# One layer of sigmoid attention and routed experts on one core: batch 6's routing moved between batch 7's two value halves, with 30 idle matmuls ahead of the last logits

## The reference, cut to what matters

```python
def reference(x, ctx_2048, g_xattn, g_ffn, norm_w, gate_w, gate_b, w1, b1, w2, b2):
    # x is (8, 256, 512): batch, rows, features; 16 experts, 4 chosen for each row
    q = _layernorm(x)
    score = sigmoid(einsum('bdn,bdm->bnm', q, ctx) / sqrt(256))
    x = x + tanh(g_xattn[0]) * einsum('bvn,bnm->bvm', ctx, score)

    y = _layernorm(x).reshape(2048, 512)
    t = y * rsqrt(mean(y * y) + EPS) * norm_w
    logits = t @ gate_w.T + gate_b
    vals, idx = top_k(logits, 4)
    G = zeros((2048, 16)).at[rows, idx].set(softmax(vals))
    h = einsum('mh,eoh->emo', t, w1) + b1
    a, b = minimum(h[..., ::2], LIMIT), clip(h[..., 1::2], -LIMIT, LIMIT)
    act = a * sigmoid(ALPHA * a) * (b + 1)
    yo = einsum('emi,edi->emd', act, w2) + b2
    return x + tanh(g_ffn[0]) * (y + einsum('me,emd->md', G, yo))
```

## Time and profile before

| what | value |
|---|---|
| median of 3 runs | 813.47 us (811.11 to 813.86) |
| the profiled execution's own time | 812.08 us |
| its span, first to last instruction | 810.3 us |
| mean granted TensorE clock | 0.976 of full speed |
| PE busy | 761.9 us, 94% of the span |
| DVE, ACT, POOL busy | 462.2, 417.3, 303.9 us |

### The profile page before, as it was taken

How to read it: one execution, slowest core, us unless ns; L and a number is a source line. 1 busy time by engine, 2 the same in 40 slices (tenths; PEclk the granted TensorE clock), 3 DMA queues, 4 the chain that set the end, 5 groups by cost and what they waited for, 6 DMA issues and landing times.

```text
span 810.3 us, 16543 instructions
## 1 busy us (share of the span) xinstructions
PE 761.9 (94%) x4067; PEld 651.7 (80%) x4068; DVE 462.2 (57%) x927; ACT 417.3 (51%) x691; POOL 303.9 (38%) x287
## 2 busy tenths in 40 slices
PE   8999996289999999999998999999999999999993
PEld 3666665168889889988888888999999889999892
DVE  3899886336556653556556553746546374735531
ACT  4567663036546554556456544646545364745531
POOL 0157767622342423341423423435333233435212
PEclk9999997599999999999999999999999999999997
DMA  8657743235757656456749654656635465654323
GB/s 285 224 186 235 243 139 117 45 105 157 168 129 209 147 147 158 94 146 200 155 128 234 170 107 136 159 140 155 155 38 151 122 168 142 168 129 77 40 26 40
DMA packets 107768, 117.02 MB, mean 144 GB/s; under 512 B 11808, under 2 KB 77344, under 8 KB 107744
## 3 DMA queue, kind: packets, MB, share of 16 engines
q1 hardware_dynamic: 88896, 77.32, 31.0%
q0 software_dynamic: 18848, 39.40, 25.1%
HBM read 88.06 MB, written 28.94 MB: 144 GB/s over the span
## 4 chain that ended last, share of the span: by engine, by line
PE 80%; DMA 5%; issue 5%; DVE 3%; POOL 3%; ACT 2%; ACTq 1%; DVEq 0%; POOLq 0%
PE ps L553 39%; PE ps L500 22%; PE ps L408 7%; PE ps L396 5%; PE ps L479 4%; DMA xg<-rows,srcI 3%; POOL tab L1181 2%; POOL out L1258 1%; PE ps L425 1%; PE ps L391 1%; PE ps L416 1%; DVE hv L1107 1%; PE ps L589 1%; DVE W1l L1116 1%; DMA ys<-rows,src 1%
## 5 line engine op out<-in xcount | busy, mean ns | idle before, releaser
L553 PE MATMUL ps<-xTh,W1h 128*128 x768 | 256.5, 334 | 4.1 <-issue 3.9
L553 PE MATMUL ps<-xTh,W1l 128*128 x768 | 250.4, 326 | 0.0
L553 PE MATMUL ps<-xTl,W1h 128*128 x768 | 250.3, 326 | 0.0
L1258 POOL DMA_INDIRECT out<-ys,dgI x75 | 118.4, 1579 | 296.4 <-ACT ys L732 277.0
L553 PEld LDWEIGHTS ps<-xTh,W1h 128*128 128x128 f32 x768 | 144.6, 188 | 11.3 <-issue 6.5
L553 PEld LDWEIGHTS ps<-xTh,W1l 128*128 128x128 f32 x768 | 144.6, 188 | 5.2
L553 PEld LDWEIGHTS ps<-xTl,W1h 128*128 128x128 f32 x768 | 144.8, 189 | 4.7
L732 ACT ACTIVATE ys<-ps,dgI 128x512 f32<-128x512 f32 x75 | 51.7, 690 | 133.3 <-DVE ps L1078 133.3
L500 PE MATMUL ps<-W2h,hTh 128*128 x288 | 112.5, 391 | 0.7 <-DVE hTl L1111 0.7
L500 PE MATMUL ps<-W2l,hTh 128*128 x288 | 112.4, 390 | 0.0
L500 PE MATMUL ps<-W2h,hTl 128*128 x288 | 112.2, 390 | 0.0
(11 more groups left out here) (153 smaller groups left out, 974.3 us busy)
## 6 DMA issues: line engine op xcount, KB each, us to landing
W1f<-in_wts SPq DMA_DIRECT2D x64, 512.0 KB, 4.7
W2f<-in_wts SPq DMA_DIRECT2D x32, 512.0 KB, 6.6
X<-in_x SPq DMA_DIRECT2D x8, 512.0 KB, 6.6
Kt<-in_ctx SPq DMA_DIRECT2D x8, 512.0 KB, 4.4
Vt<-in_ctxT SPq DMA_DIRECT2D x8, 512.0 KB, 4.5
rows<-tt SPq DMA_DIRECT2D x8, 512.0 KB, 3.0
out<-base SPq DMA_DIRECT2D x8, 512.0 KB, 2.9
b2s<-in_bias SPq DMA_DIRECT2D x16, 256.0 KB, 8.4
```

Of the source, the lines that this page charges most:

```text
L553: m = e.matmul(P_[i % 2][:, 0:32 * w], (W1h, W1l)[wl][:, i, 2 * k + h, :], (xTh, xTl)[xl][:, bass.ds(par, 1), k, 0:32 * w], start=(t == 0) ...
L1258: e.indirect_dma_start(out, bass.IndirectOffsetOnAxis(dgI[:, j, 0:1].bitcast(I32), axis=0), ys[j][:], None, compute_op=ALU.add).then_inc(d ...
```

## The change

On PE, `av` may now be issued in parts, and the last batch is written out: `av(7, 0)` is split around `turn_t(6)`, `logits(6)` follows it, then three of the four matmuls of `av(7, 1)`, `rank(6)`, the fourth matmul, and 30 idle matmuls ahead of `turn_t(7)`. On ACT, `out_base(6)` goes behind `keep_tT(6)`. On DVE, `choose(6)`, `gates(6)` and `places(6)` go between the two tiles of batch 7. On POOL, the first two of `put(6)`'s eight DMAs go ahead of `x1_scale(7)`.

```diff
-            def av(b, j):
-                if j == 0:
+            def av(b, j, cs=range(4)):
+                if j == 0 and cs[0] == 0:
                     e.wait_ge(d_v[b % 2], 16 * (b // 2 + 1))
                 if b >= 1:
                     e.wait_ge(v_x1, 2 * (b - 1) + j + 1)
-                for c in range(4):
+                for c in cs:
                     if j == 0:
                         e.wait_ge(a_sig, 4 * b + c + 1)
                     m = e.matmul(ps[2 + j][:], Vt[b % 2][:, c, 128 * j:128 * j + 128], Sc[:, c, :], start=(c == 0), stop=(c == 3))
-                m.then_inc(t_av, 1)
+                if cs[-1] == 3:
+                    m.then_inc(t_av, 1)
...
                 qk(b, 3)
+                if b == B - 1:
+                    break
                 av(b, 0)
...
+            av(B - 1, 0, range(2))
+            turn_t(B - 2, 0)
+            turn_t(B - 2, 1)
+            av(B - 1, 0, range(2, 4))
+            logits(B - 2)
+            av(B - 1, 1, range(3))
             rank(B - 2)
+            av(B - 1, 1, range(3, 4))
+            run_idle(30)
             turn_t(B - 1, 0)
             turn_t(B - 1, 1)
             logits(B - 1)
...
-                if b >= 1:
+                if 1 <= b < B - 1:
                     out_base(b - 1, 0)
                     out_base(b - 1, 1)
...
+            out_base(B - 2, 0)
+            out_base(B - 2, 1)
             gate_sigmoids(B - 2)
...
                     if j == 0 and b + 1 < B:
                         low_q(b + 1)
+                    elif j == 0:
+                        choose(B - 2)
+                        gates(B - 2)
+                        places(B - 2)
                 x1_var(b)
-            choose(B - 2)
-            gates(B - 2)
-            places(B - 2)
             base_scale(B - 1)
...
-            def put(b):
+            def put(b, qs=range(2 * K)):
...
-                for q in range(2 * K):
+                for q in qs:
...
+            put(B - 2, range(2))
             x1_scale(B - 1)
-            put(B - 2)
+            put(B - 2, range(2, 2 * K))
             put(B - 1)
```

## The result

| | before | changed |
|---|---|---|
| median | 813.33 us (811.11 to 813.86, 4 runs) | 819.37 us (818.65 to 821.70, 4 runs) |
| ratio | 1 | 1.0078 (95% interval 1.0051 to 1.0106) |
| profiled execution: time, span | 812.08, 810.3 us | 818.65, 816.9 us |
| mean granted TensorE clock | 0.976 | 0.981 |
| PE busy | 761.9 us | 773.6 us |

The change makes the kernel 6.0 us slower; 818.8 us was forecast, with 6.2 us on the path. A later group of runs gave the same ratio, 1.0079 (1.0061 to 1.0097), with 816.90 us against 810.34. All later runs were made in three groups, each beside its own runs of the kernel before (811.15, 810.34 and 810.90 us); each is compared with those of its own group, not with 813.33.

What follows compares the result with a forecast made beforehand. PE is 94% busy; the last put, behind batch 7's path and POOL's queue, sets stage two's start. 2.5 (scaling) + 6.1 (idle matmuls) - 2.2 (warm clock) = +6.4, less up to 0.46: +6.2 on 812.6, 818.8 us; range 815.5 to 822.0.

Steps and rivals of the forecast that it cites:

- transposes could have started: On PE, batch 7's transposes have their scaled input at 137.16 us instead of 134.65, because x1_scale(7) starts 2.5 us later.
- The idle matmuls: On PE, 30 calls of 0.433 us take 13.0 us; 14 exceed the gap and delay batch 7's transposes by 6.1 us.
- Rival A: On PE, idle calls cost up to 0.22 us and just fill the gap: -0.1 to +0.3 us, 812.7 us; chance 0.07.
- the gap figure of the Trainium skill: 0.109 us for a warm 256-column matmul on PE; 30 would take 3.3 or 6.6 us and fit the gap.
- Batch 7's logits: On PE, from first transpose to choose(7) takes 3.25 us at warm clock against 5.48 cold, giving back 2.2 us.
- POOL: Put(6) begins at 133.0 instead of 135.50, but two of its puts delay x1_scale(7) by 2.5 us to 135.24.
- The two bounds of put(7): Batch 7's gates (145.33) and POOL's end of put(6) (145.38) lie close, so shortening POOL's queue alone gains nothing.
- Rival D: At the start of stage two, a wait not moving with the table swallows part: +3 to +4.5, 816 us; chance 0.04.

Runs made afterwards that it cites:

- e8: The changed kernel itself run and profiled again, nothing altered: 816.90 us against 810.34, ratio 1.0079.
- e1: The changed kernel without its 30 idle matmuls, the moved routing kept: 812.25 us against 811.15, ratio 1.0011.
- e2: The changed kernel with 15 idle matmuls instead of 30: 810.95 us against 811.15, ratio 0.9986.
- e3: The changed kernel with 45 idle matmuls instead of 30: 1159.19 us, ratio 1.427.
- e6: The kernel before, order kept, with 8 idle matmuls ahead of rank(6) and 3 behind it: 809.42 us against 810.34, ratio 0.9993.
- e4: The kernel before with only 30 idle matmuls added between rank(6) and batch 7's transposes: 821.38 us against 811.15, ratio 1.0123.
- e7: The changed kernel with tile 1's value matmuls together, 14 idle matmuls, one put ahead of x1_scale(7), gates(7) ahead of places(7): 808.83 us, ratio 0.9986.
- e9: The changed kernel with 30 idle matmuls of 16 columns instead of 30 of 256: 819.88 us, ratio 1.0108.
- e10: The changed kernel with 94 idle matmuls of 16 columns instead of 30 of 256: 845.61 us, ratio 1.0425.
- e5: The changed kernel with 45 idle matmuls of 16 columns instead of 30 of 256: 1149.15 us, ratio 1.418.

## Why the prediction was right

By its own steps, with the second profile of the changed kernel (e8):

| step | predicted | measured |
|---|---|---|
| idle block | 130.34 to 143.3 | 130.35 to 143.31 |
| price of a call | 0.433 us | 0.432 us |
| transposes could have started | 137.16 | 136.68 (e1) |
| choose(7) starts | 146.55 | 146.64 |
| put(6) ends, then POOL waits | 143.9, 8 us | 143.34, 8.78 us |
| put(7) starts later by | 6.0 to 6.4 | 6.04 |
| SP loads the table | 163 | 163.07 |
| time | +6.2 | +6.04 and +6.56 (medians, two groups) |

**The idle matmuls** were the term that decided, and its row was the one that was read right: the start of the next group, not the number of records. Rival A (a call at half its price, the block over before 137.16) is excluded by 0.432 us a call in e2, e3 and e8. By the same rows the gap figure of the Trainium skill ("TensorE: Matmul & The Clock Gate", section "Back-to-back issue gap") does not hold for these float32 calls.

**Batch 7's logits** came back by 2.2 us with the warm clock as forecast: e1 shows 1.97 and 3.57, e2 1.10 and 1.93 for the same transposes and logits at the same place, which start at 136.68 and 136.67, and put(7) starts 2.18 us earlier in e2.

**POOL** was mis-sized by a little. The step "POOL is through with put(5) at 132.71" took over a date from the kernel before; in the changed order it was 131.97 (e8 has the eighth put at 131.02, for 0.95). The second put of batch 6 then took 1.19 instead of 0.96, and `x1_scale(7)` started at 134.75 instead of 135.24. The transposes' input was ready 0.5 us earlier than I said. It changed nothing, since the idle block covered it, but without the block the moved routing cost 1.6 us at put(7), not the 2.1 to 2.5 of e1's expectation.

**The two bounds of put(7)** are shown by e6 (gates at 142.6, put(7) at 145.53) and by the changed kernel (put(6) ends at 143.3, put(7) at 152.12). The 0.29 to 0.75 us from gates to put was 0.76 (gates end at 151.13 + 0.23).

**Rival D, part of the shift is swallowed,** was given 0.04 and is half true: the mechanism is there, the forecast had put it at nothing ("Nothing in the rows shows such a wait"), and the medians did not follow it. In e8 the first transposes of stage two start 6.36 us later than before, and the first matmul of the loop 4.86 later (174.86 against 170.00). The rows of the kernel before and of e8, from their timelines of PE:

```profile
170.00 0.47 PE L553 MATMUL ps<-xTh,W1h 128*128 x1 [1.60 <-issue]
```

```profile
174.86 0.46 PE L564 MATMUL ps<-xTh,W1h 128*128 x1 [0.27 <-DVE xTl L1067]
```

The kernel before has a pause of 1.60 us there that the changed one has not. e6 has it too (1.41), and e1 one of 0.98; the nine other traces wait 0.26 or 0.27 us there. The three with the pause are those with 0 or 11 idle calls, and the others have 14 or more. What the instruction queue did fits that. Its row in the kernel before, for 166.5 to 167.0 us:

```profile
q8 instruction: 1, 0.02, 15.2%
```

So a packet of instructions starts some 3 us ahead of the loop's first matmul, and so it does in e6 (between 166.0 and 166.5, matmul at 169.31) and e1 (168.0 and 168.5, matmul at 171.26). In the other nine traces no packet starts in the 13 us up to 0.3 us ahead of that matmul. The pause does not go with the routing: e1 has the moved routing and the pause, e4 the old routing and none. It goes with the place of the code, as e3's loss does; that PE waits there for this packet is argued from the dates, and no run tested it.

It bears on every difference of about a microsecond in this document. In e2 the table is loaded at 157.31, 0.3 us later than before, and the loop starts at 169.11, 0.9 us earlier: the small gain of e2 is the pause that is gone, and not an earlier table. Of e7's gain some 1.3 us are the same.

So that the time came out at +6.2 is in part luck. The path to the table was +6.03 as forecast, then the pause took 1.3 us of it back, and the loop of e8 started 4.86 us late; that execution took 816.15 us, 4.1 more than the profiled one before. The medians still say +6.04 and +6.56; where in stage two the difference of 1.2 to 1.7 us comes from was not found. Waits on gathered rows differ by some tenths of a microsecond from execution to execution (one at 441.52 was 2.24 us in the kernel before, 1.45 in the changed one). The profiled execution with the three pauses had put(7) 8.4 us late and ended 6.6 us late.

## What to carry to other kernels

Size a block of idle matmuls by the gap that it is to fill and by the start-to-start time of such a call in the same trace, at the clock that it will have there; records can be two to a call. Whatever is too long stands in front of the work that it was meant to speed up. Where a path and a queue end within a microsecond of each other, as batch 7's gates and POOL's puts here, the one alone gains next to nothing (e6), and moving the other first makes a new wait. And look at the instruction queue's packets after any edit that lengthens straight code ahead of a loop: their number, and whether one starts just ahead of the loop. A difference of a microsecond can be the code's place and not the edit's purpose.

## What the runs showed of the hardware that was not expected

- The place of PE's loop in its code can cost 43%: 45 idle calls ahead of it gave 1159 and 1149 us, 30 and 94 gave 816 to 846 us, with 210 instruction packets against 12 and 13.
- Ahead of the loop's first matmul PE pauses for 0.98 to 1.60 us in just those three of twelve traces in which a packet of instructions starts some 3 us before it (0.26 or 0.27 us in the others).
- Idle calls of 16 columns saved little time and did not hold the clock here: 0.35 us a call, the weight loads busy all the time, PE busy without a gap, and a granted clock of 0.50, where calls of 256 columns in the same place cost 0.43 us and ran at 1.00.
- PE pauses of 0.2 to 1.0 us with no cause in the profile came up between 136 and 147 us in three of the seven executions with a block of 30 calls or more (the first of the changed kernel, e9, e10), and not in e3, e4, e5 and e8. They are open.
